# First attention: weighing of values ahead of the scores in steps 6 and 12 to 15

## What is computed

```python
qkv = hidden_states @ Wqkv_w.T + Wqkv_b                 # 16 query, 8 key heads of 128; pairs of them
p1 = attn_map(q[:, :, :, 0], k[:, :, :, 0])             # causal softmax(q k / sqrt(128)), 1024 x 1024
p2 = attn_map(q[:, :, :, 1], k[:, :, :, 1])
p = p1 - lam * p2
o = jnp.einsum('bhqk,bkhe->bqhe', p, v)                 # v has 256 columns
o = o * rms(o) * subln_w * (1 - LAMBDA_INIT)
return o.reshape(B, S, H * D) @ out_w.T + out_b
```

## Time and profile before

| what | value |
| --- | --- |
| median of 3 runs | 1719.83 us (1718.26 to 1720.5) |
| profiled execution, its own time | 1719.16 us |
| its span | 1717.3 us |
| busy in the span: TensorE, VectorE, ScalarE, POOL | 1626.5, 1133.5, 929.4, 581.0 us |
| TensorE's granted clock, mean of the span | 0.994 |
| the first attention's weighing of values | first starts at 61.3 us, last at 1291.1 us, four groups in each of two batches |

### The profile page before, as it was taken

How to read it: one execution, slowest core, us unless ns; L and a number is a source line. 1 busy time by engine, 2 the same in 40 slices (tenths; PEclk the granted TensorE clock), 3 DMA queues, 4 the chain that set the end, 5 groups by cost and what they waited for, 6 DMA issues and landing times.

```text
span 1717.3 us, 33139 instructions
## 1 busy us (share of the span) xinstructions
PE 1626.5 (95%) x11040; PEld 1406.8 (82%) x11040; DVE 1133.5 (66%) x2654; ACT 929.4 (54%) x1942; POOL 581.0 (34%) x518
## 2 busy tenths in 40 slices
PE   4999999999999899899989999999999989999998
PEld 3888989889888677688878889898988877767887
DVE  6667667667645778455776676776755477765567
ACT  3565556565444577543356665656554337773343
POOL 2554435544560102011126355443555420030120
PEclk8999999999999999999999999999999999999999
DMA  4100000000120423101010000000002123221110
GB/s 129 41 26 16 26 1 15 24 16 2 38 67 11 75 47 71 49 28 47 10 51 17 25 16 26 16 16 8 17 2 65 39 40 66 49 55 44 38 47 25
DMA packets 35211, 60.16 MB, mean 35 GB/s; under 512 B 7988, under 2 KB 22068, under 8 KB 33768
## 3 DMA queue, kind: packets, MB, share of 16 engines
q1 hardware_dynamic: 35064, 58.28, 12.9%
HBM read 42.24 MB, written 3.42 MB: 27 GB/s over the span
## 4 chain that ended last, share of the span: by engine, by line
PE 69%; DVE 11%; ACT 8%; issue 7%; POOL 2%; SPq 1%; DMA 1%; ACTq 0%; DVEq 0%; POOLq 0%
PE ps L349 17%; PE ps L351 16%; PE ps L350 16%; PE ps L931 4%; PE ps L988 4%; PE ps L971 4%; PE ps L783 2%; ACT E L1177 2%; DVE nmax L1488 2%; POOL E L1818 1%; ACT PT_h L1159 1%; PE ps L967 1%; DVE On L1430 1%; PE ps L720 1%; POOL E L1815 1%
## 5 line engine op out<-in xcount | busy, mean ns | idle before, releaser
L1177 ACT ACTIVATE E<-ps,nmax 128x128 f32<-128x128 f32 (+7 forms) x256 | 189.0, 741 | 207.2 <-DVE nmax L1488 206.7
L1815 POOL TENSOR_SCALAR E<-E,mixc 128x128 f32<-128x128 f32 (+7 forms) x128 | 97.2, 759 | 381.9 <-DVE mixc L1458 381.9
L1488 DVE TENSOR_REDUCE nmax<-ps 128x1 f32<-128x128 f32 (+7 forms) x256 | 183.3, 749 | 13.1 <-PE ps L758 13.0
L1818 POOL TENSOR_TENSOR E<-E 128x128 f32<-128x128 f32 (+7 forms) x128 | 182.4, 1425 | 10.7
L1284 ACT ACTIVATE PT<-ps 128x512 f32<-128x512 f32 x288 | 154.5, 601 | 57.8 <-PE ps L971 55.4
L1801 POOL TENSOR_TENSOR Fw_l<-Fw_raw,Fw_h 128x768 fp32r<-128x768 f32 x48 | 88.5, 1844 | 253.5 <-ACT Fw_h L1224 252.7
L349 PE MATMUL ps<-V_h,PT_h 128*128 128x256 f32 x576 | 166.9, 290 | 0.0
L351 PE MATMUL ps<-V_h,PT_l 128*128 128x256 f32 x576 | 162.7, 282 | 0.0
L350 PE MATMUL ps<-V_l,PT_h 128*128 128x256 f32 x576 | 162.7, 282 | 0.0
L349 PE MATMUL ps<-XT_h,Fw_h 128*128 128x512 f32 x384 | 153.0, 398 | 3.5 <-DVE XT_l L1361 3.5
L349 PE MATMUL ps<-K_h,Q_h 128*128 128x512 f32 (+3 forms) x384 | 147.7, 385 | 7.2 <-ACT E L1177 4.2
(11 more groups left out here) (213 smaller groups left out, 4660.3 us busy)
## 6 DMA issues: line engine op xcount, KB each, us to landing
Fw_raw<-in_fa SPq DMA_DIRECT2D x48, 256.0 KB, 2.7
Wa_raw<-in_wa SPq DMA_DIRECT2D x9, 1024.0 KB, 4.9
Wo_raw<-in_wo SPq DMA_DIRECT2D x8, 512.0 KB, 3.5
Fw_raw<-in_fb SPq DMA_DIRECT2D x32, 128.0 KB, 2.7
KS<-QK_h SPq DMA_DIRECT2D x56, 64.0 KB
QS<-QK_h SPq DMA_DIRECT2D x56, 64.0 KB
Xn<-in_x SPq DMA_DIRECT2D x3, 1024.0 KB, 5.8
Fw_raw<-w2s SPq DMA_DIRECT2D x16, 128.0 KB, 2.7
```

What stands on the lines that cost most here:

```text
L1177: nc.scalar.activation(e[:, 0:w], ps[m][:, 0:w], ACT.Exp, bias=nmax[:, s % 4, m:m + 1], accum_out=lsum[:, s % 4, m:m + 1]).then_inc(exp_do ...
L1488: nc.vector.tensor_reduce(nmax[:, s % 4, m:m + 1], ps[m][:, 0:(s % NT + 1) * P], AX.X, ALU.max, negate=True).then_inc(nmax_ready[m], 1)
L1815: nc.gpsimd.tensor_scalar(e2, e2, mixc[:, n % 4:n % 4 + 1], 1.0, ALU.mult, ALU.mult).then_inc(mix_scaled, 1)
L1818: nc.gpsimd.tensor_tensor(e1, e1, e2, ALU.add).then_inc(p_ready, 1)
```

## The change

A tuple of steps replaces the single step 8. In these steps TensorE weighs W(s - 3) ahead of the scores S(s), and VectorE takes O(s - 3) ahead of the maxima M(s). Step 8 keeps its order; steps 6, 12, 13, 14 and 15 get the same. On ScalarE only the place of `project_out(s, 0)` moves.

```diff
+VALUES_FIRST = (6, NT, *range(NT + 4, STEPS0))
@@ tensor, attn0_group
-                if s != NT:
+                if s not in VALUES_FIRST:
                     scores(s)
                 for t in v_tiles(s) if s else ():
                     project0(it, UNITS0 + t)
                 project_out(s, 0)
                 if s >= 3:
                     weigh_values(s - 3)
-                if s == NT:
+                if s in VALUES_FIRST:
                     scores(s)
                 project_out(s, 1)
@@ scalar, attn0_group
-                if s == NT:
+                if s in VALUES_FIRST:
                     project_out(s, 0)
                 for m, e in ((0, E1[s % 2]), (1, E2[s % 2])):
-                    if m == 1 and s != NT:
+                    if m == 1 and s not in VALUES_FIRST:
                         project_out(s, 0)
```

## The result

The changed kernel takes 1746.28 us, median of 4 runs (1745.99 to 1746.63), beside 1719.05 us for the kernel before on the same chip: ratio 1.0159, 95% interval 1.0141 to 1.0177. It is slower by 27.2 us where 23.2 was forecast.

The account below looks back on a forecast made before the run. TensorE, busy 1626.5 of 1717.3 us, was taken as level with a slackless VectorE and ScalarE loop in steps 12 to 15. 1719.83 + 11.4 (steps 12 to 15) + 11.8 (step 6) = 1743.0 us; overall range 1729 to 1752.

Parts of the forecast that it names:

- What bounds: Steps 12 to 15: VectorE and ScalarE loop without slack, 4.61 us a turn, level with TensorE's work of 4.69 us.
- Step 6: Weighing ahead delays the scores, nothing taken back: 1.5 us in six groups, 1.4 in two, 11.8 us in all.
- Step 12: Weighing fills TensorE's wait for the previous group's last output tile, yet maxima end 0.26 us later in groups having that wait.
- Steps 13 to 15: Later maxima make the transposes of P wait for POOL; 1.2 us lost in each of four groups followed by another.
- The last groups: Last group of each batch: clock-keeping matmuls and step 15's transposes wait for P(14)'s low part, 1.8 us late, two such.
- everything of TensorE's clock stays as it is: Steps 12 to 15: TensorE's granted clock remains at 1.00, as before, with waits up to 1.6 us there.
- The sum: Whole kernel: 11.4 us for steps 12 to 15 plus 11.8 us for step 6, giving 1743.0 us.
- VectorE's exchange: Eviction between low part and maxima in five steps: costs 0.40 us per loop turn, zero where maxima await scores; no gain.
- Rival A: Steps 12 to 15: VectorE evicts in idle time, weighing covers TensorE's waits; 8.3 us faster, 1711.5 us; chance 0.06.
- B: Steps 8 to 11: their waits absorb step 6's loss in six groups, up to 9.0 us, giving 1734 us; chance 0.17.
- C: Steps 6 and 12 to 15: both losses vanish under TensorE's full queue, giving 1720 us; chance 0.05.
- D: Each of eight groups loses 1 us more, through projections after step 14's transposes or step 7's maxima: 1751 us; chance 0.10.

Follow-up runs that it names:

- The fill: Changed kernel with six clock-keeping matmuls of 512 columns added in the last group of each batch, in TensorE's wait for the low part of P(14): 1742.54 us, ratio 1.0135.

## Why the prediction was right, point by point

- What bounds: right. The loop of exponentials, cast, low part and maxima is level with TensorE in the wide steps. Work taken out of it won 11.5 us, work put into it cost 27.3, with TensorE untouched. But "level" holds for two chains: in steps 12 to 14 the relieved loop won only 0.1 us a group, and with it relieved the exchange still costs 28.7 us.
- Step 6: right, 11.8 forecast, 12.7 by the stretches (1.5 to 1.7 a group where 1.5 and 1.4 were taken). Nothing behind it gave it back. The forecast that T(6) waits for POOL holds only in the two first groups (0.35 us by the starts).
- Step 12: right in its sign and nearly in size: 0.19 us with the wait filled, 0.26 forecast; 0.45 in the first groups. The time of that run alone would not have shown it.
- Steps 13 to 15: right. T(12), T(13) and T(14) wait 1.26, 0.53 and 0.41 us by the starts, forecast 1.4, 0.5 and 0.4; to the next group's projection +1.26, forecast 1.2.
- The last groups: the mechanism was right, the size was not. The chain's part is 0.96 us to T(14) and 0.81 to T(15), 1.8 as forecast, as the run with steps 12 to 15 alone shows. The full change took 3.1 and 2.8. The sentence "everything of TensorE's clock stays as it is" was the step that failed. Its ground was misread: the stretch of the earlier trace rows holds no wait over 0.40 us; the wait of 1.6 us is that of T(7) in the first group, and behind the same wait in the fifth group, 1.56 us, the kernel before did lose the clock. The fill gave 2.3 us of it back by the stretches. Why the same wait let the clock fall in the full change and not in the run with steps 12 to 15 alone (1.76 us there too) is open.
- The sum: 23.2 forecast, 27.2 measured. Step 6 was sized 0.9 us too low, the two last groups 2.3 (the clock) and the stretch behind the first of them 0.3; the rest is under 0.1 us a group. The sign "TensorE's busy time stays near 1626" did not come true (1634.0).
- VectorE's exchange: half wrong, without harm to the sum. "No gain can come from it" was read from the old order, in which nobody waited for O. In the new order W(s-2) does. The price of 0.40 us a turn is in the trace (4.61 to 5.00 us), but leaving O where it was costs 8.5 us more.
- Rival A, faster: fell. M(13) starts 0.6 us later behind T(10) than before (7.12 and 6.54 us), and no wait of TensorE in these steps became shorter but that for X. The rule of the Trainium skill ("Perfetto Trace Analysis", Identifying the Most-Contended Engine, with Optimization Strategy behind it) led to it: to improve the engine with the highest occupancy first and to find its gaps and what they wait for. That page does not say to fill them with other work, which is what this change did. Here the fill for X was worth nothing, and the gain of 11.5 us came from an engine busy 54% of the time.
- Rivals B, C and D fell: the waits of steps 8 to 11 stand as they did, and beside the clock no group lost a further microsecond.

## What to carry to other kernels

When an engine with 95% occupancy waits here and there, follow the chain behind its next products before filling a gap with work that is ready: what matters is when the block that others wait for ends, not when the engine is busy. Find the loop across engines whose steps join without a gap, and test it by moving or adding half a microsecond in it; work that has no user near (the squares here) belongs where that engine waits anyway. When blocks are swapped on one engine, look again at which buffers they now reuse sooner, and swap their readers with them.

## What the hardware showed

- The granted clock fell to 1.2 GHz now and then in a program that otherwise keeps 2.4 GHz in the first attention. In the last groups this turned a loss of 1.8 us into 3.1 and 2.8. Where it happens differs from trace to trace: behind the wait of T(7) in the fifth group of the kernel before, in the first group with step 12 alone, in neither in the changed one, though there this wait is longer (1.81 and 1.80 us). So the length of a wait alone does not tell. Differences of 1 or 2 us between such kernels are better read from repeated stretches than from the medians.
- Without POOL's scaling, steps 0 to 4 became 1.0 us longer in the groups that project outputs, and in no others. VectorE's normalisation of an output tile (SBUF to SBUF) in the kernel before, and then in that kernel with POOL's sum beside it:

```profile
148.91 0.85 DVE L1430 TENSOR_SCALAR On<-O,orstd 128x256 f32 x2
152.05 0.61 DVE L1430 TENSOR_SCALAR On<-O,orstd 128x256 f32 x2
...
177.62 1.81 DVE L1430 TENSOR_SCALAR On<-O,orstd 128x256 f32 x2
...
176.62 2.40 POOL L1818 TENSOR_TENSOR E<-E 128x1024 f32<-128x1024 f32 x1
```

```profile
149.31 1.10 DVE L1430 TENSOR_SCALAR On<-O,orstd 128x256 f32 x2
152.72 1.40 DVE L1430 TENSOR_SCALAR On<-O,orstd 128x256 f32 x2
...
149.38 0.89 POOL L1815 TENSOR_TENSOR E<-E 128x256 f32<-128x256 f32 x1 [0.61 <-DVE mixc L1458]
152.95 1.01 POOL L1815 TENSOR_TENSOR E<-E 128x384 f32<-128x384 f32 x1 [1.27 <-DVE mixc L1458]
```

  Two of them take 1.10 and 1.40 us and not 0.85 and 0.61, and end 0.15 us behind POOL's sum (150.41 and 150.27; 154.12 and 153.96). That the two engines exclude each other there is what the Trainium skill says of their shared port pair ("SBUF — State Buffer", Who interferes with whom); the trace agrees. The two rows are 0.25 and 0.79 us longer, together the 1.0 us. So an earlier POOL instruction can make a kernel slower. The same stands in the kernel before: in step 8 the pair at 177.62 takes 1.81 us beside POOL's sum of E(7), and M(8) starts 2.46 us behind the pair's start. Without the scaling the pair stands at 179.03, 0.19 us before that sum ends; it takes 0.61 us, M(8) starts 1.70 us behind it, and TensorE's wait for On (the 3.5 us of the earlier trace rows, six times before T(8)) is gone from its list. This fits the 0.68 us won from T(7) to T(8).
